# Attention on one Trainium2 core: weighing two quarters of a unit at a time, in even steps only, and both score halves ahead of the copies on VectorE

## The chip, the cores and the metric

The kernel runs on one core of one Trainium2 chip. The metric is the device time of one execution in microseconds; less is better. Times below come from three unprofiled runs and from one profiled execution.

## The reference, cut to what matters

The reference is one transformer block over `x` (2 x 2048 x 512) with 16 heads of 32, followed by a small rotation. Nearly two thirds of the device time, and all of the change, lie in its attention:

```python
scores = jnp.einsum('bhqd,bhkd->bhqk', q / math.sqrt(HEAD_DIM), k)
scores = scores + attention_bias                 # (2, 16, 2048, 2048) float32, read once
scores = jnp.where(src_mask, -jnp.inf, scores)   # keys that are padding
probs = jax.nn.softmax(scores, axis=-1)
ctx = jnp.einsum('bhqk,bhkd->bhqd', probs, v)
```

The layer norm and the projections of q, k and v stand ahead of it; the output projection, the feed-forward part and the rotation behind it.

## The kernel before

The program is three blocks, one after the other: `phase_a` (layer norm, projections), `phase_b` (attention) and `phase_c` (the rest). Only `phase_b` is touched.

**Tiles.** A tile is 128 queries of one head against all 2048 keys: a 128 x 2048 block of scores, 1 MB, whose bias is read from HBM straight into one of eight slots of `ring`. A trip has eight tiles, one for each slot, and there are 64 trips: 512 tiles. Four tiles (512 queries of one head) are a unit. Every engine has its own instruction stream, written out by hand as `step(it, j)`: trip `it`, slot `j` from 0 to 7, tile `i = it * 8 + j`. The first trip and one behind the last are unrolled; the rest is a loop over trips. Steps with even `j` are called even here, the others odd.

**What happens to a tile.**
1. SyncE loads its bias into the ring slot, as soon as the slot's last user has been turned (L450).
2. GpSimd adds the mask penalty to the first 1856 columns in place (L478). The last 192 columns get theirs from TensorE, by a matmul with the identity (L627).
3. TensorE, step `i`: scores of the tile in two halves of 1024 columns, two matmuls for each half (L621), into the PSUM tiles `scores0` and `scores1`.
4. VectorE, step `i`: `add(it, j, 0)` and `add(it, j, 1)` (L542) add each half of the scores to the ring slot and keep the row's extreme, first in `low_part`, then in `low`. The second half reads the first's `low_part`, and waits for it by the semaphore `added`.
5. ScalarE, step `i + 1`: the exponential over 2048 columns, in place (L574).
6. TensorE, step `i + 2`: the exponentials are turned (transposed) in 16 blocks of 128 x 128, four blocks to a **quarter**, in `turn(it, j, n)` for quarters n = 0 to 3 (L655). Three PSUM banks serve four quarters: an even tile uses banks 0, 1, 2, 0, an odd one 2, 1, 0, 2. So quarter 3 always needs the bank of quarter 0 of its own tile back.
7. The turned quarters are copied from PSUM to `probT`: quarters 0 and 1 by ScalarE, behind the exponential of its step (L584), quarters 2 and 3 by VectorE (L526).
8. **Weighing** (L678): when a unit's four tiles are in `probT`, its product with the values is made, `weigh(it, j)`, in four parts. One part is four matmuls of 128 x 32 against 512 columns, which run side by side on four strips of the array (the profile counts each float32 matmul twice, so a part is 8 there). The result gathers in `bank_ctx`, which ScalarE copies out to `ctxp` (L590) and stores.

**The order around the change.** TensorE's step is: scores of half 0, of half 1, turns 0 and 1, one part of the weighing, turns 2 and 3. Waits stand ahead of the instruction that needs them, some of them a block or two early. Those that matter here:
- the last score matmul of a half waits, for half 0, for the exponential of tile `i - 2` (semaphore `exp_done`), and for half 1 for VectorE's copy of quarter 2 of the tile before (`out_dve`);
- the first score matmul of a half waits for the add of that half of tile `i - 1` (`added`);
- `turn(it, j, 2)` waits at its first block for the copy of quarter 3 of the tile before (`out_dve`), and ahead of its third block for ScalarE's copy of quarter 0 of its own tile (`pe.wait_ge(out_act, t * 2 + 1)`), since quarter 3 goes into that bank.

VectorE's step is: add half 0, copy quarter 3 of tile `i - 3`, add half 1, copy quarter 2 of tile `i - 2`. ScalarE's is: exponential of tile `i - 1`, copies of quarters 0 and 1 of tile `i - 2`, and in steps 1 and 5 of a trip the copy of `bank_ctx`. Step 0 of a trip puts a small copy of `low` in front (L573).

Of the kernel before, what the change touches and what calls it, by code (L numbers as in the profile page):

```python
# [27 lines left out]
P = 128  # L28
B, S, D, F = 2, 2048, 512, 2048
H = 16  # L30
DH = D // H
# [3 lines left out]
QT = TOK // P  # L35
# [5 lines left out]
R = 2 * QT  # L41
# [334 lines left out]
def phase_b(nc, sem, side, q_rows, k_rows, v_heads, pen_scratch, ctx_scratch, ident, sums_all, low_all):  # L376
# [9 lines left out]
    QR = KB // 4  # L386
# [4 lines left out]
    UNITS = TRIPS * 2  # L391
    assert QR * P == N
    with ExitStack() as ctx:
# [33 lines left out]
        ctx_stored = sem("ctx_stored")  # L427

        SCORED0, TURNED0, PV0 = 2 * R * CH, 4 * R, 2

        block = ctx.enter_context(nc.Block())

# [74 lines left out]
        def column(all_tiles, it, j):  # L507

            if known(it):
                return all_tiles[:, it, j:j + 1]  # L510
            return all_tiles[:, bass.ds(it, 1), j:j + 1].rearrange("p o n -> p (o n)")

        @block.vector
        def _(dve):
            nc.vector.tensor_copy(identb[:], ident[:]).then_inc(identb_ready, 1)

            def copy_quarter(it, j, n, lag):

                t, k = it * R + j - lag, (j - lag) % R
                hh, q = k // QT, k % QT  # L520
                if live(t, NT):
                    dve.wait_ge(turned, TURNED0 + t * 4 + n + 1)
                    if q == 0 and n == 2:

                        dve.wait_ge(pv_done, PV0 - 1 + (it * 2 if j == 2 else it * 2 + 1))
                    nc.vector.tensor_copy(probT[:, hh, QR * n:QR * (n + 1), q * P:(q + 1) * P],  # L526
                                          turn_bank(k, n)[:].rearrange("p (c q) -> p c q", c=QR)).then_inc(out_dve, 1)

            def add(it, j, c):

                i = it * R + j
                if live(i, NT):
                    dve.wait_ge(scored, SCORED0 + i * CH + c + 1)
                    if c == 0:
                        dve.wait_ge(masked, i + 1)
                    else:
                        dve.wait_ge(added, i * CH + c)
                        if j == 0:
                            need(dve, low_kept, it)
                    dve.nop(nofuse=True)  # L540
                    at = ring[:, j, c * CW:(c + 1) * CW]
                    nc.vector.tensor_tensor_reduce(out=at, in0=scores[c][:], in1=at, scale=-1.0,  # L542
                                                   scalar=low_part[:, j:j + 1] if c else -MASKED,
                                                   op0=ALU.add, op1=ALU.min,
                                                   accum_out=low[:, j:j + 1] if c else low_part[:, j:j + 1]).then_inc(added, 1)

            def step(it, j):
                add(it, j, 0)
                copy_quarter(it, j, 3, 3)
                add(it, j, 1)  # L550
                copy_quarter(it, j, 2, 2)

            trips(dve, step)

        @block.scalar
        def _(act):
            def load_values(it, hh):
                batch, h = it // (TRIPS // B), it % H
                act.dma_start(values[:, hh, :, :].rearrange("p k d -> p (k d)"),
                              v_heads[bass.ds(batch * H + h, 1)].rearrange("o p n -> (o p) n")).then_inc(v_in[hh], 16)  # L560

            act.sem_inc(ctx_stored, 16)
            load_values(0, 0)
            load_values(0, 1)

            def step(it, j):
                i = it * R + j
                if live(i - 1, NT):
                    k, trip = (j - 1) % R, it if j else it - 1
                    act.wait_ge(added, i * CH)  # L570
                    if j == 0:

                        nc.scalar.copy(low_all[:, bass.ds(trip, 1), :].rearrange("p o n -> p (o n)"), low[:]).then_inc(low_kept, 1)  # L573
                    nc.scalar.activation(ring[:, k, :], ring[:, k, :], ACT.Exp, bias=low[:, k:k + 1], scale=-1.0,  # L574
                                         accum_out=column(sums_all, trip, k)).then_inc(exp_done, 1)
                if live(i - 2, NT):
                    k = (j - 2) % R
                    hh, q = k // QT, k % QT
                    for n in (0, 1):
                        act.wait_ge(turned, TURNED0 + (i - 2) * 4 + n + 1)  # L580
                        if q == 0 and n == 0:

                            act.wait_ge(pv_done, PV0 - 1 + (it * 2 if j == 2 else it * 2 + 1))
                        nc.scalar.copy(probT[:, hh, QR * n:QR * (n + 1), q * P:(q + 1) * P],  # L584
                                       turn_bank(k, n)[:].rearrange("p (c q) -> p c q", c=QR)).then_inc(out_act, 1)
                unit, hh = closing(it, j), 0 if j < QT else 1
                if j % QT == 1 and live(unit, UNITS):
                    act.wait_ge(pv_done, PV0 + unit + 1)
                    act.wait_ge(ctx_stored, unit * 16 + 16)
                    nc.scalar.copy(ctxp[:], bank_ctx[:]).then_inc(ctx_copied, 1)  # L590
                    if not known(it) or it < TRIPS:
                        load_values(it, hh)
                if j % QT == 2 and live(unit, UNITS):
                    trip = it - 1
                    act.wait_ge(ctx_copied, unit + 1)
                    act.dma_start(ctx_scratch[bass.ds((trip // H) * 2 * H + hh * H + trip % H, 1)].rearrange("o p n -> (o p) n"),
                                  ctxp[:]).then_inc(ctx_stored, 16)

            trips(act, step)

        @block.tensor
        def _(pe):
# [28 lines left out]
            def free_before_turn(it, j, c):  # L631

                t = it * R + j - 2
                if live(t, NT):
                    if c == 0:
                        pe.wait_ge(exp_done, t + 1)
                    else:
                        need(pe, out_dve, t * 2 - 1)

            def turn(it, j, n):  # L640

                t, slot = it * R + j - 2, (j - 2) % R
                if n == 2 and live(t, NT):
                    need(pe, out_dve, t * 2)
                for c in range(QR):
                    if c == 2:
                        if n == 0 and live(t, NT):
                            need(pe, out_act, t * 2)
                        if n == 1:
                            copied_before_weigh(it, j)  # L650
                        if n == 2 and live(t, NT):
                            pe.wait_ge(out_act, t * 2 + 1)
                    if live(t, NT):
                        at = (QR * n + c) * P
                        last = nc.tensor.transpose(turn_bank(slot, n)[:, c * P:(c + 1) * P], ring[:, slot, at:at + P], ident[:])  # L655
                if live(t, NT):
                    last.then_inc(turned, 1)

            def weighed(it, j):
                unit = it * 2 - 2 if j < 2 else it * 2 - 1 if j < 6 else it * 2  # L660
                return (j - 2) % QT, unit, 1 if 2 <= j < 6 else 0

            def copied_before_weigh(it, j):

                n, unit, hh = weighed(it, j)
                if live(unit, UNITS):
                    pe.wait_ge(out_act if n < 2 else out_dve, (unit * QT + QT - 1) * 2 + n % 2 + 1)

            def weigh(it, j):


                n, unit, hh = weighed(it, j)
                if live(unit, UNITS) and n == 0:
                    pe.wait_ge(v_in[hh], it * 16 if j == 2 else it * 16 + 16)
                    need(pe, ctx_copied, unit)
                for c in range(4):
                    if live(unit, UNITS):
                        last = nc.tensor.matmul(bank_ctx[DH * c:DH * (c + 1), :], values[:, hh, QR * n + c, :],  # L678
                                                probT[:, hh, QR * n + c, :], start=(n == 0), stop=(n == 3))
                if live(unit, UNITS) and n == 3:  # L680
                    last.then_inc(pv_done, 1)

            def step(it, j):
                score(it, j, 0)
                score(it, j, 1)
                turn(it, j, 0)
                turn(it, j, 1)
                weigh(it, j)
                turn(it, j, 2)
                turn(it, j, 3)  # L690

            trips(pe, step)
# [427 lines left out]
```

## Time and profile before

| | |
|---|---|
| median of three runs | 3677.97 us (3676.59 to 3677.99) |
| the profiled execution | 3678.13 us |
| its span, first to last instruction | 3676.1 us |
| first to last step of the attention on VectorE | 521.4 to 2545.4 us |
| busy in the span: PE / PEld / DVE / ACT / POOL | 3436.5 / 1956.3 / 2488.7 / 1893.6 / 2077.3 us |

PE is TensorE's matmul side, PEld its weight loads, DVE is VectorE, ACT is ScalarE, POOL is GpSimd, SP is SyncE. L with a number is a line of the kernel before. In a timeline row the first number is when the first instruction of a merged group starts, the second how long the group lasts; in brackets is the idle time of the engine ahead of it and what ended that. Ends of matmuls are modelled by the profiler, so starts are the safer numbers.

### The profile page before, as it was taken

The numbers are of one execution on the slowest core, as the hardware profiler recorded it, in microseconds if no ns is written. First come the engines' busy times: TensorE is split into PE (matmuls) and PEld (weight loads), VectorE is DVE, ScalarE is ACT, GpSimd is POOL, SyncE is SP. The second block draws the span as 40 slices with busy tenths as digits, with TensorE's granted clock in tenths as the row PEclk, the third lists the DMA queues.
The fourth block names the chain that finished last, engine by engine and source line by source line (L and its number), as shares of the span: only waits on it lengthen the run. The fifth ranks groups of instructions, "written<-read, shape, count | busy, mean of one in ns | idle before, by whom it ended". The sixth has DMA issues, their size and how long they took to land. (4 is left out here: it accounts for less than half of the span.)

```text
span 3676.1 us, 61259 instructions
## 1 busy us (share of the span) xinstructions
PE 3436.5 (93%) x18338; PEld 1956.3 (53%) x18338; DVE 2488.7 (68%) x4176; ACT 1893.6 (52%) x2544; POOL 2077.3 (57%) x642
## 2 busy tenths in 40 slices
PE   6787779999999999999999999998499999999997
PEld 2333336666666666666666666665244444444443
DVE  3444449999999999999999999997333424434332
ACT  2212228888888888888888888886111111111110
POOL 0000039999999999899999899996112202201100
PEclk9898889999999999999999999999799999999999
DMA  6787789999999999999999999996612202201100
GB/s 235 231 262 249 242 311 373 349 344 347 352 394 348 352 344 351 374 367 350 343 348 350 394 348 350 349 346 218 181 42 69 69 0 68 68 19 49 46 12 12
DMA packets 291097, 906.13 MB, mean 246 GB/s; under 512 B 94208, under 2 KB 94208, under 8 KB 214272
## 3 DMA queue, kind: packets, MB, share of 16 engines
q1 hardware_dynamic: 238976, 805.14, 61.4%
q10 hardware_dynamic: 49536, 92.29, 7.3%
q0 software_dynamic: 2560, 8.39, 0.6%
q8 instruction: 12, 0.20, 0.0%
q14 instruction: 13, 0.11, 0.0%
HBM read 763.12 MB, written 142.61 MB: 246 GB/s over the span
## 5 line engine op out<-in xcount | busy, mean ns | idle before, releaser
L478 POOL TENSOR_TENSOR ring<-ring,penb 128x1856 f32<-128x1856 f32 x512 | 1904.0, 3756 | 629.3 <-DMA penb<-pen_scratch 543.6
L574 ACT ACTIVATE ring<-ring,low 128x2048 f32<-128x2048 f32 x512 | 1028.7, 2009 | 317.4 <-DVE low L542 317.4
L655 PEld LDWEIGHTS b_T<-ident,ring 128*128 128x128 f32 x8192 | 890.4, 141 | 429.7 <-DVE probT L526 426.6
L655 PE MATMUL b_T<-ident,ring 128*128 128x128 f32 x8192 | 1091.8, 276 | 2.6 <-DVE probT L526 2.6
L542 DVE CUSTOM_DVE_ANT_0 ring<-scores,ring 128x1024 f32<-128x1024 f32 x512 | 627.2, 1225 | 176.8 <-PE scores L621 154.8
L526 DVE COPY probT<-b_T 128x512 f32<-128x512 f32 x1024 | 702.6, 686 | 4.9 <-PE b_T L655 4.8
L542 DVE CUSTOM_DVE_ANT_0 ring<-scores,ring,low_part 128x1024 f32<-128x1024 f32 x512 | 652.8, 1275 | 0.4
L621 PE MATMUL scores<-keys,queries 128*128 (+1 forms) x2048 | 621.7, 425 | 21.0 <-DMA queries<-q_rows 16.6
L678 PE MATMUL bank_ctx<-probT,values 128*32 128x512 f32 x4096 | 544.9, 604 | 0.0
L584 ACT COPY probT<-b_T 128x512 f32<-128x512 f32 x1024 | 538.0, 575 | 3.0 <-PE b_T L655 3.0
L845 POOL TENSOR_TENSOR y_out<-rot_a,rot_b 128x512 f32<-128x512 f32 x32 | 41.6, 1299 | 785.9 <-DVE rot_b L1003 785.9
L897 ACT ACTIVATE gate<-c_up,b_scaled 128x512 f32<-128x512 f32 x128 | 87.9, 687 | 741.1 <-PE c_up L1054 741.0
L1054 PE MATMUL c_up<-hT,w 128*128 (+1 forms) x1024 | 459.1, 592 | 0.7 <-ACT hT L889 0.7
L1064 PE MATMUL c_acc<-w,hidden 128*128 128x512 f32 x1024 | 458.9, 592 | 0.0
L621 PEld LDWEIGHTS scores<-keys,queries 128*128 128x128 f32 x2048 | 347.5, 190 | 143.6 <-DVE probT L526 74.2
L984 DVE SCALAR_TENSOR_TENSOR hidden<-c_up,b_col,gate 128x512 f32<-128x512 f32 x128 | 96.0, 750 | 393.3 <-ACT gate L897 376.5
L1064 PEld LDWEIGHTS c_acc<-w,hidden 128*128 128x128 f32 x1024 | 194.0, 190 | 241.6 <-issue 241.6
L1054 PEld LDWEIGHTS c_up<-hT,w 128*128 128x128 f32 x1024 | 190.7, 190 | 222.0 <-issue 221.0
L233 ACT ACTIVATE std<-mean_var,eps_a 128x4 f32<-128x4 f32 x8 | 2.4, 297 | 314.6 <-DVE mean_var L303 314.6
L838 POOL TENSOR_TENSOR parts<-parts 128x1024 f32<-128x1024 f32 x30 | 72.6, 2419 | 158.8 <-DMA parts<-ctx_scratch 158.7
L328 DVE TENSOR_SCALAR exact<-a_G,bias_col 128x512 f32<-128x512 f32 x64 | 48.1, 751 | 153.2 <-PE a_G L370 153.2
L1035 PE MATMUL c_fore<-wo,ctxT 128*128 128x512 f32 x256 | 116.7, 601 | 18.2 <-DVE ctxT L937 18.2
(101 smaller groups left out, 1940.2 us busy)
## 6 DMA issues: line engine op xcount, KB each, us to landing
ring<-in_fside_Bx16xSxS SPq DMA_DIRECT2D x512, 1024.0 KB, 7.5
keys<-k_rows SPq DMA_DIRECT2D x64, 1024.0 KB, 8.6
values<-v_heads ACTq DMA_DIRECT2D x128, 256.0 KB, 5.3
queries<-q_rows SPq DMA_DIRECT2D x128, 256.0 KB, 8.0
ctx_scratch<-ctxp ACTq DMA_DIRECT2D x128, 256.0 KB, 6.6
parts<-ctx_scratch SPq DMA_DIRECT2D x128, 256.0 KB, 4.9
k_rows<-part_hi SPq DMA_DIRECT2D x64, 256.0 KB, 2.9
k_rows<-part_lo SPq DMA_DIRECT2D x64, 256.0 KB, 2.9
```

Of the source, the lines that this page charges most:

```text
L478: nc.gpsimd.tensor_tensor(ring[:, j, 0:POOL_MASKED], ring[:, j, 0:POOL_MASKED], penb[:, j, 0:POOL_MASKED], ALU.add).then_inc(masked, 1)
L526: nc.vector.tensor_copy(probT[:, hh, QR * n:QR * (n + 1), q * P:(q + 1) * P], turn_bank(k, n)[:].rearrange("p (c q) -> p c q", c=QR)).then ...
L542: nc.vector.tensor_tensor_reduce(out=at, in0=scores[c][:], in1=at, scale=-1.0, scalar=low_part[:, j:j + 1] if c else -MASKED, op0=ALU.add, ...
L574: nc.scalar.activation(ring[:, k, :], ring[:, k, :], ACT.Exp, bias=low[:, k:k + 1], scale=-1.0, accum_out=column(sums_all, trip, k)).then_ ...
L584: nc.scalar.copy(probT[:, hh, QR * n:QR * (n + 1), q * P:(q + 1) * P], turn_bank(k, n)[:].rearrange("p (c q) -> p c q", c=QR)).then_inc(ou ...
L621: last = nc.tensor.matmul(scores[c][:, n * N:(n + 1) * N], queries[:, hh, q * P:(q + 1) * P], keys[:, bass.ds(it % 2, 1), c * CW + n * N:c ...
L655: last = nc.tensor.transpose(turn_bank(slot, n)[:, c * P:(c + 1) * P], ring[:, slot, at:at + P], ident[:])
L678: last = nc.tensor.matmul(bank_ctx[DH * c:DH * (c + 1), :], values[:, hh, QR * n + c, :], probT[:, hh, QR * n + c, :], start=(n == 0), sto ...
L984: nc.vector.scalar_tensor_tensor(out=hidden[:, f % 4, :], in0=up[f % 2][:], scalar=b1_col[:, f:f + 1], in1=gate[:, f % 2, :], op0=ALU.add, ...
L1035: last = nc.tensor.matmul(fore[t % 2][:], ctxT[:, c, t * P:(t + 1) * P], wo[:, c, :], start=(c == 0), stop=(c == DB - 1))
L1054: last = nc.tensor.matmul(up[f % 2][:], w1[:, c, f * P:(f + 1) * P], hT[:, bass.ds(u % 2, 1), c, :].rearrange("p o n -> p (o n)"), start=( ...
L1064: last = nc.tensor.matmul(acc[t][:], hidden[:, k % 4, t * P:(t + 1) * P], w2[:, k, :], start=(k == 0), stop=(k == FB - 1))
```

## The change

Three things move; what is computed stays the same.

- **Weighing.** `weigh` is called in even steps only, between `turn(it, j, 2)` and `turn(it, j, 3)`, and does two parts (16 matmuls in the profile's count) at once. Slots 2 and 6 do parts 0 and 1 of a unit, slots 4 and 0 do parts 2 and 3. The waits for it move into quarter 2's turn, ahead of its third block.
- **VectorE** does `add` of half 0, `add` of half 1, then copies quarter 2 and quarter 3, both of tile `i - 2`. Nothing stands between the two adds any more, and quarter 3 is copied one step earlier than before.
- **ScalarE** has its copies in a helper of its own; its order is unchanged.

```diff
@@ VectorE
             def step(it, j):
                 add(it, j, 0)
-                copy_quarter(it, j, 3, 3)
                 add(it, j, 1)
-                copy_quarter(it, j, 2, 2)
+                copy_quarter(it, j, 2)
+                copy_quarter(it, j, 3)
@@ TensorE, in turn(it, j, n)
                     if c == 2:
                         if n == 0 and live(t, NT):
                             need(pe, out_act, t * 2)
-                        if n == 1:
+                        if n == WEIGH_AFTER and j % 2 == 0:
                             copied_before_weigh(it, j)
                         if n == 2 and live(t, NT):
                             pe.wait_ge(out_act, t * 2 + 1)
@@ TensorE, the weighing
+                unit, hh, n = weighed(it, j)
                 if live(unit, UNITS):
-                    pe.wait_ge(out_act if n < 2 else out_dve, (unit * QT + QT - 1) * 2 + n % 2 + 1)
+                    if n == 0:
+                        pe.wait_ge(v_in[hh], it * 16 if j == 2 else it * 16 + 16)
+                        need(pe, ctx_copied, unit)
+                    pe.wait_ge(out_act if n == 0 else out_dve, (unit * QT + QT) * 2)
...
+                unit, hh, first = weighed(it, j)
+                for n in (first, first + 1):
+                    for c in range(4):
+                        if live(unit, UNITS):
+                            last = nc.tensor.matmul(bank_ctx[DH * c:DH * (c + 1), :], values[:, hh, QR * n + c, :],
+                                                    probT[:, hh, QR * n + c, :], start=(n == 0), stop=(n == 3))
@@ TensorE, step
                 turn(it, j, 0)
                 turn(it, j, 1)
-                weigh(it, j)
                 turn(it, j, 2)
+                if j % 2 == 0:
+                    weigh(it, j)
                 turn(it, j, 3)
```

TensorE, step 2 of a trip in the loop, from the second block of turn 1 on, before. L655 are the turns with the bank they write, L678 the weighing, L621 the next step's scores; names in brackets are the semaphores that an instruction waits for.

```order
L655 MATMUL b_T1<-ident,ring 128x128 x2
L667 ISA
L655 MATMUL b_T1<-ident,ring 128x128 [waits out_act]
L655 MATMUL b_T1<-ident,ring 128x128
L678 MATMUL bank_ctx<-probT,values 32x512 [waits ctx_copied,v_in1]
L678 MATMUL bank_ctx<-probT,values 32x512 x3
L655 MATMUL b_T2<-ident,ring 128x128 [waits out_dve]
L655 MATMUL b_T2<-ident,ring 128x128
L652 REGISTER_ALU
L655 MATMUL b_T2<-ident,ring 128x128 [waits out_act]
L655 MATMUL b_T2<-ident,ring 128x128
L655 MATMUL b_T0<-ident,ring 128x128 x4
```

The same place with the change (its lines are some ten higher: L664 the turns, L688 the weighing):

```order
L664 MATMUL b_T2<-ident,ring 128x128 [waits out_dve]
L664 MATMUL b_T2<-ident,ring 128x128
L491 REGISTER_ALU [waits v_in1]
L680 ISA [waits ctx_copied]
L661 REGISTER_ALU [waits out_act]
L664 MATMUL b_T2<-ident,ring 128x128 [waits out_act]
L664 MATMUL b_T2<-ident,ring 128x128
L688 MATMUL bank_ctx<-probT,values 32x512 x8
L664 MATMUL b_T0<-ident,ring 128x128 x4
```

The weighing is now eight matmuls in one piece, and the wait for ScalarE's copy of quarter 0, which stood behind the weighing, stands ahead of it.

VectorE, one step of the loop before (L542 the adds, L526 the copies):

```order
L535 REGISTER_ALU [waits scored]
L542 ISA ring,low_part<-scores0,ring 128x1024 [waits masked]
L542 ISA low_part 128x1
L522 REGISTER_ALU
L526 COPY probT<-b_T0 128x4x128 [waits turned]
L533 REGISTER_ALU
L537 REGISTER_ALU [waits scored]
L542 ISA ring,low<-scores1,ring,low_part 128x1024 [waits added]
L542 ISA low 128x1
L522 ISA
L526 COPY probT<-b_T0 128x4x128 [waits turned]
```

The same with the change (L543 the adds, L527 the copies):

```order
L536 REGISTER_ALU [waits scored]
L543 ISA ring,low_part<-scores0,ring 128x1024 [waits masked]
L543 ISA low_part 128x1
L534 REGISTER_ALU
L538 REGISTER_ALU [waits scored]
L543 ISA ring,low<-scores1,ring,low_part 128x1024 [waits added]
L543 ISA low 128x1
L523 ISA
L527 COPY probT<-b_T0 128x4x128 [waits turned]
L523 REGISTER_ALU
L527 COPY probT<-b_T2 128x4x128 [waits turned]
```

The copy that stood between the two adds now stands last, and the second of the copies waits for a quarter that TensorE turns, in even steps, behind the weighing of the same step.

## Rows read from the trace of the kernel before

**Rows 1.** Windows in the attention: length, busy (count) by engine, PEclk, DMA share, GB/s

```profile
1000.00:1500.00 500.00, 500.00 (x3673) 322.91 (x3665) 460.63 (x760) 406.56 (x554) 470.16 (x127) 1.00 0.96 357
2000.00:2500.00 500.00, 500.00 (x3673) 322.96 (x3666) 460.60 (x760) 406.49 (x555) 469.83 (x127) 1.00 0.96 356
```

**Rows 2.** Line L542 on VectorE: duration ns min/median/max, first and last start us

```profile
L542 DVE CUSTOM_DVE_ANT_0 ring<-scores,ring x512: 1224/1225/1227, 521.4 to 2543.7; 128x1024 f32<-128x1024 f32 x171
```

**Rows 3.** Waits by releaser, 1000 to 2500 us: us in total, times, longest

```profile
PEld b_T L655 <- DVE probT L526: 318.6, 380, 0.8
ACT ring L574 <- DVE low L542: 224.1, 333, 0.9
DVE ring L542 <- PE scores L621: 106.8, 343, 0.4
POOL ring L478 <- DMA ring<-in_fside_Bx16xSxS: 63.3, 58, 2.6
PEld scores L621 <- DVE probT L526: 54.9, 285, 0.2
```

**Rows 4.** Timeline of one step, all engines: start us, us, what [idle before]

```profile
1505.97 1.28 DVE L542 CUSTOM_DVE_ANT_0 ring<-scores,ring,low_part 128x1024 f32<-128x1024 f32 x1
...
1507.17 0.69 DVE L526 COPY probT<-b_T 128x512 f32<-128x512 f32 x1
...
1507.29 1.18 PE L621 MATMUL scores<-keys,queries 128*128 x4
1507.38 2.01 ACT L574 ACTIVATE ring<-ring,low 128x2048 f32<-128x2048 f32 x1 [0.77 <-DVE low L542]
...
1508.23 1.23 DVE L542 CUSTOM_DVE_ANT_0 ring<-scores,ring 128x1024 f32<-128x1024 f32 x1 [0.38 <-PE scores L621]
...
1508.31 0.26 PE L627 MATMUL scores<-penb,identb 128*128 128x192 bf16 x1
...
1508.41 1.04 PE L655 MATMUL b_T<-ident,ring 128*128 128x128 f32 x8
...
1509.37 1.07 PE L678 MATMUL bank_ctx<-probT,values 128*32 128x512 f32 x8
1509.38 1.05 ACT L584 COPY probT<-b_T 128x512 f32<-128x512 f32 x2
...
1509.38 0.69 DVE L526 COPY probT<-b_T 128x512 f32<-128x512 f32 x1
1509.98 1.28 DVE L542 CUSTOM_DVE_ANT_0 ring<-scores,ring,low_part 128x1024 f32<-128x1024 f32 x1
1510.37 0.86 PEld L655 LDWEIGHTS b_T<-ident,ring 128*128 128x128 f32 x8 [0.84 <-DVE probT L526]
1510.37 1.09 PE L655 MATMUL b_T<-ident,ring 128*128 128x128 f32 x8
...
1511.18 0.69 DVE L526 COPY probT<-b_T 128x512 f32<-128x512 f32 x1
...
1511.22 1.21 PE L621 MATMUL scores<-keys,queries 128*128 x4
```

**Rows 5.** The same timeline, the next step's last score load and what follows it

```profile
1511.92 0.19 PEld L621 LDWEIGHTS scores<-keys,queries 128*128 128x128 f32 x1 [0.20 <-DVE probT L526]
...
1512.27 0.10 PEld L627 LDWEIGHTS scores<-penb,identb 128*128 128x128 bf16 x1 [0.16 <-issue]
```

**Rows 6.** Timeline of VectorE in the first trip, where no copy is due between the adds

```profile
531.36 1.22 DVE L542 CUSTOM_DVE_ANT_0 ring<-scores,ring 128x1024 f32<-128x1024 f32 x1 [1.10 <-issue]
532.51 0.08 DVE L542 DVE_READ_ACCUMULATOR2_ANT low_part<- 128x1 f32 x1
532.73 1.28 DVE L542 CUSTOM_DVE_ANT_0 ring<-scores,ring,low_part 128x1024 f32<-128x1024 f32 x1
```

**Rows 7.** Groups by line, whole execution: busy us, mean ns | idle before

```profile
L584 ACT COPY probT<-b_T 128x512 f32<-128x512 f32 x1024 | 538.0, 575 | 3.0 <-PE b_T L655 3.0
L573 ACT COPY low_all<-low 128x8 f32 x64 | 12.6, 198 | 59.2 <-DVE low L542 59.2
L478 POOL TENSOR_TENSOR ring<-ring,penb 128x1856 f32<-128x1856 f32 x512 | 1904.0, 3756 | 629.3 <-DMA penb<-pen_scratch 543.6 <-DMA ring<-in_fside_Bx16xSxS 83.0
```

**Rows 8.** Timeline at the attention's end: several weighing parts in one piece, loads of each four

```profile
2554.45 0.13 PEld L678 LDWEIGHTS bank_ctx<-probT,values 128*32 128x32 f32 x4 [0.30 <-issue]
...
2556.60 0.13 PEld L678 LDWEIGHTS bank_ctx<-probT,values 128*32 128x32 f32 x4 [0.30 <-issue]
```

More of the change, by code:

```diff
@@ L429, in phase_b @@
         SCORED0, TURNED0, PV0 = 2 * R * CH, 4 * R, 2
+        WEIGH_AFTER = 2
         block = ctx.enter_context(nc.Block())
@@ L515, in _, with copy_quarter @@
             nc.vector.tensor_copy(identb[:], ident[:]).then_inc(identb_ready, 1)
-            def copy_quarter(it, j, n, lag):
-                t, k = it * R + j - lag, (j - lag) % R
+            def copy_quarter(it, j, n):
+                t, k = it * R + j - 2, (j - 2) % R
                 hh, q = k // QT, k % QT
@@ L564, in _, with exponentials @@
             load_values(0, 1)
-            def step(it, j):
+            def exponentials(it, j):
                 i = it * R + j
@@ L575, in step, with copy_quarter @@
                                          accum_out=column(sums_all, trip, k)).then_inc(exp_done, 1)
+            def copy_quarter(it, j, n):
+                i = it * R + j
                 if live(i - 2, NT):
@@ L578, in step @@
                     hh, q = k // QT, k % QT
[L579 to L585, printed above, removed]
+                    act.wait_ge(turned, TURNED0 + (i - 2) * 4 + n + 1)
+                    if q == 0 and n == 0:
+                        act.wait_ge(pv_done, PV0 - 1 + (it * 2 if j == 2 else it * 2 + 1))
+                    nc.scalar.copy(probT[:, hh, QR * n:QR * (n + 1), q * P:(q + 1) * P],
+                                   turn_bank(k, n)[:].rearrange("p (c q) -> p c q", c=QR)).then_inc(out_act, 1)
+            def step(it, j):
+                exponentials(it, j)
+                copy_quarter(it, j, 0)
+                copy_quarter(it, j, 1)
                 unit, hh = closing(it, j), 0 if j < QT else 1
@@ L636, in free_before_turn @@
                         pe.wait_ge(exp_done, t + 1)
-                    else:
+                    if c == 1:
                         need(pe, out_dve, t * 2 - 1)
@@ L660, in weighed @@
                 unit = it * 2 - 2 if j < 2 else it * 2 - 1 if j < 6 else it * 2
-                return (j - 2) % QT, unit, 1 if 2 <= j < 6 else 0
+                return unit, 1 if 2 <= j < 6 else 0, 0 if j % QT == 2 else 2
             def copied_before_weigh(it, j):
-                n, unit, hh = weighed(it, j)
+                unit, hh, n = weighed(it, j)
                 if live(unit, UNITS):
-                    pe.wait_ge(out_act if n < 2 else out_dve, (unit * QT + QT - 1) * 2 + n % 2 + 1)
+                    if n == 0:
+                        pe.wait_ge(v_in[hh], it * 16 if j == 2 else it * 16 + 16)
+                        need(pe, ctx_copied, unit)
+                    pe.wait_ge(out_act if n == 0 else out_dve, (unit * QT + QT) * 2)
             def weigh(it, j):
[L672 to L680, printed above, removed]
+                unit, hh, first = weighed(it, j)
[4 more added lines that the diff above has]
+                                                    probT[:, hh, QR * n + c, :], start=(n == 0), stop=(n == 3))
+                if live(unit, UNITS) and first == 2:
                     last.then_inc(pv_done, 1)
```

## The prediction

> **What bounds the kernel now.** The chain that ended last lies wholly in the last third, so for the attention I go by windows, waits and one step of the timeline. The windows [rows 1] show the attention steady: matmuls in progress all the time, VectorE 0.92 busy, GpSimd 0.94, the DMA engines 0.96, TensorE's clock at 1.00 of full speed, that is 2.4 GHz. The first adds run from 521.4 to 2543.7 us, 512 of them [rows 2], so a step takes 2022.3 / 511 = 3.96 us. The single step shown [rows 4] takes 3.93, from scores at 1507.29 to scores at 1511.22. In it TensorE has no gap: scores 1.02 us (to 1508.31), the masked columns 0.10, eight turns 0.96, the weighing 1.00, eight turns 0.85. The wait "PEld on DVE, 0.84" ahead of the second turns [rows 3, 4] is no loss: VectorE's copy of 1509.38 ended at 1510.07, and the loads began at 1510.37, when the matmuls of the weighing were through. A true wait is the load of the last score matmul at 1511.92, 0.05 us behind the end (1511.18 + 0.69) of VectorE's copy [rows 4, 5]. It costs little: from scores to masked columns takes 1.05 us there and 1.02 in the step before. So TensorE bounds, by a small margin: GpSimd needs 3.76 us a step [rows 7], and 0.96 of 3.96 us is 3.80 for the DMA.
>
> What matters next is how near the other loop is, in which the same engines wait for each other. For two steps it now reads: scores to first add 0.94 (1507.29 to 1508.23), first to second add 1.75 (1508.23 to 1509.98), second add to exponential 1.41 (1505.97 to 1507.38), exponential to the first copy 2.00, the copy 0.57 [rows 7] and 0.05 to TensorE, which then may make the third block of quarter 2 and five more, some 0.64, and start scores. That is 7.36 us in two steps of 7.91, so 0.55 of slack. The trace agrees: ScalarE's copy ended at 1509.38 + 0.57 = 1509.95, and its quarter's third block was due near 1510.5.
>
> **TensorE alone.** Of two steps with 2 x 1.00 us of weighing one block of 1.86 stays: 1.00 for the first part, and 2 x 0.43 for the second, since in the pile at the end six groups of four loads start 2554.45 to 2556.60, 0.43 apart [rows 8]. With one entry and one restart less (eight turns up to the weighing take 0.96 where seven spacings of 0.11 are 0.77; eight behind it last 1.09, others 1.04) two steps save about 0.14 + 0.19 - 0.11 + 0.06 = 0.28 us. By itself that would be 0.14 us a step.
>
> **VectorE's order.** Four instructions a step as before. Between the adds no copy hides the wait for `low_part`. In the first trip no copy was due there: 531.36 to 532.73, 1.37 us [rows 6], of which 1.15 is up to the reading of the accumulator. With the copy between it is 1.75, so the second add, and the exponential behind it, come 0.38 earlier. The price is 0.22 us of idle VectorE, whose own step becomes 1.37 + 1.20 + 0.60 + 0.60 = 3.77 us, still below 3.96. By the Trainium skill (VectorE: DVE Perf Modes, "The DRAIN you can't avoid") a semaphore between VectorE's operations costs nothing extra. Then first to second add would be 1.15, and the forecast below 56 us less. The row shows 1.37, and it decides.
>
> **The loop that I expect to bind.** TensorE obeys its waits in program order. In an even step the third block of quarter 2 still waits for ScalarE's copy of quarter 0, and that wait now stands ahead of the weighing, of quarter 3 and of the next step's scores. ScalarE makes that copy behind the exponential of the preceding odd step's tile, which needs that tile's adds, and those need its scores, which TensorE starts only when the even step before is through. Over a pair, from the odd step's scores to the next odd step's:
> - scores to first add 0.94, first to second add 1.37 [rows 4, 6];
> - second add to exponential 1.41, exponential to copy 2.00, copy 0.57, to TensorE 0.05 [rows 4, 5, 7];
> - two turns and the entry of the weighing: 0.96 for eight less six at 0.11, and 0.05 for the restart, 0.35;
> - the weighing, two parts: 1.86;
> - quarter 3 and the way to the scores: 0.85 for eight less four at 0.11, 0.41.
>
> Sum 8.96, and 0.05 for the copy of `low` (0.20 once in four pairs) [rows 7]: 9.01 us a pair, 4.50 a step. The adds came 0.38 earlier, but 1.86 + 0.41 of TensorE stand where 0.64 stood. 256 pairs x 9.01 = 2307 us against 512 x 3.96 = 2027 now: +280. The profiled execution took 3678.13 us, within 0.2 of the median, so 3958 us. All other edits cost nothing: ScalarE's order is the same, `bank_ctx` is finished a step earlier, quarter 3's copy is asked for a step later, and VectorE's wait for quarter 3 in even steps (it comes at the step's end) is covered, since its next add has to wait 0.94 us for scores and the copy takes 0.60 until the next start. GpSimd and the DMA will have slack: 3.76 and 3.80 of 4.50.
>
> **Bounds.** First to second add: the lower end is 1.15 (no price at all, -56 us), the upper 1.75 (as now with a copy, +97); I take 1.37, the same two instructions in this order. The waits in the loop read registers, which in the first trip were constants, so a little more is likelier than less. The weighing: 4 x 0.43 = 1.72 at least (-36), 2 x 1.00 at most (+36). The two ends far out seldom meet; that gives 3870 to 4020 for this case.
>
> **Rivals.**
> 1. **Only the bank loop binds.** If the wait for quarter 0's copy does not hold back the weighing (it is met earlier than I think, or does not keep the later matmuls), the next loop goes through VectorE: scores to first add 0.94, 1.37, add to copy of quarter 2 1.20, copy 0.69 and 0.05, load of the last score matmul to the masked columns 0.35 [rows 5], 0.10, twelve turns 0.96 + 0.44, weighing 1.86, 0.41: 8.37 us a pair, 4.19 a step, +116: 3794 us. For it: ScalarE has 0.55 us of slack today. Against: that slack is smaller than the 1.6 us that the even step adds. The Trainium skill (TensorE: Matmul & The Clock Gate, "The mechanism") has matmuls start strictly in order, only loads run ahead; by that the weighing can't pass the waiting turn. 7 in 100.
> 2. **TensorE stays the bound, and it gets faster.** The place is the same wait. If ScalarE's copy of quarter 0 lands before the third block of quarter 2 in every even step, two steps cost 7.91 - 0.28 and some 0.03 for the score wait that goes: 7.60, or 3.80 a step, where the DMA's 3.80 also stands, -81: 3597 us. For it: the exponential starts 0.38 us earlier. Against: the loop of 9.01 us would have to be 1.4 shorter; it decides at 7.91, and no term is doubtful by so much. 6 in 100. No change at all would need the loops to meet 7.91 by chance: 1 in 100.
> 3. **The clock falls too.** TensorE would stand idle some 1.4 of 9 us. The clock is 1.00 in the steady windows, which have no pause [rows 1], so they do not show what pauses do. Were a fifth of the attention at the 1.2 GHz level, TensorE's 3.6 us on the loop (0.94, 0.35, 1.86 and 0.41) would double there: 256 x 0.2 x 3.6 = +184 on top, some 4140 us. 4 in 100.
>
> **The numbers.** Likeliest case 82 in 100, 3958 us. The range 3860 to 4020 holds nearly all of it, some 80 in 100; the rivals stay outside. A measurement of this kernel tells about 0.2% from no change. Faster by more 0.06, within 0.01, slower 0.93.
>
> **What will show it.** Odd steps' scores to even steps' about 2.9 us, even to odd about 6.1 in place of 3.96 each. TensorE waits for ScalarE's `probT` copies some 0.5 us or more in each even step, a wait that is absent now, and for VectorE at the even steps' scores. First to second add 1.37 us. GpSimd idle waiting for the ring, DMA share near 0.84. It is wrong if steps alternate without a wait for ScalarE's copies (rival 1 or 2), or if the clock leaves 1.00 (rival 3).

## The result and the profile after

The changed kernel takes 3960.4 us (median of four runs, 3959.2 to 3963.57) against 3678.0 for the kernel before: ratio 1.077, 95% interval 1.0751 to 1.0789. The forecast was 3958. The whole loss lies in the attention. Its first adds on VectorE, one a tile, run from 521.6 to 2825.1 us, which is 2303.5 us where it was 2022.3 [rows 2]: 281 of the 282 us.

```profile
L543 DVE CUSTOM_DVE_ANT_0 ring<-scores,ring x512: 1212/1224/1226, 521.6 to 2825.1; 128x1024 f32<-128x1024 f32 x171
```

By the same figures the attention was 55% of the execution of the kernel before, less than the nearly two thirds named at the top.

A window in the attention of the changed kernel (length, busy and count of PE, PEld, DVE, ACT, POOL, then PEclk, DMA share, GB/s):

```profile
1000.00:1500.00 500.00, 470.66 (x3218) 288.70 (x3219) 410.84 (x665) 360.04 (x485) 413.09 (x112) 1.00 0.81 313
```

Against [rows 1] every engine does less in the same time: 112 bias tiles pass GpSimd in 500 us where 127 did, and the busy time of VectorE, ScalarE, GpSimd and the weight loads falls in about that ratio, by 11 or 12%. TensorE's matmul side counts 3218 matmuls for 3673, but its busy time falls by 6% only, because matmuls that wait for their loads count as in progress: the scores at 1501.85 below last 1.76 us, those at 1507.81 1.18. The clock stays at 1.00. No engine bounds; they wait for each other. Its waits in the attention, 1000 to 2500 us (us in total, times, longest):

```profile
POOL ring L479 <- DMA ring<-in_fside_Bx16xSxS: 232.5, 148, 3.3
DVE probT L527 <- PE b_T L664: 217.0, 167, 1.4
...
PEld b_T L664 <- ACT probT L588: 149.6, 333, 0.7
PEld b_T L664 <- issue: 140.0, 167, 0.8
...
PE b_T L664 <- ACT probT L588: 67.4, 167, 0.5
...
PEld scores L630 <- DVE probT L527: 52.1, 125, 0.4
PEld scores L630 <- DVE low L543: 47.1, 125, 0.4
```

Of [rows 3] the turns' wait of 0.84 us for VectorE, which the weighing's matmuls had filled, is still there behind each weighing: 167 times instead of 380, now put down to "issue", and no loss now either. What is new is that TensorE's loads wait for ScalarE's copies, 333 times, once in each step, and that in every second step (167 times) the matmul side itself runs dry, for 0.40 us. The largest wait, GpSimd's for the bias, is a result and no cause: its slots are loaded again only when TensorE has turned them, and it falls to 141.2 us in e1 below, where only a wait of TensorE is moved.

One pair of steps in the timeline, all engines (start us, us, what; in brackets the idle time before and what ended it). The odd step's scores are at 1498.83, the even step's at 1501.85, the next odd step's at 1507.81:

```profile
1498.83 0.70 PE L630 MATMUL scores<-keys,queries 128*128 x2
...
1499.77 1.23 DVE L543 CUSTOM_DVE_ANT_0 ring<-scores,ring 128x1024 f32<-128x1024 f32 x1
...
1501.15 1.28 DVE L543 CUSTOM_DVE_ANT_0 ring<-scores,ring,low_part 128x1024 f32<-128x1024 f32 x1
1501.21 0.64 PEld L664 LDWEIGHTS b_T<-ident,ring 128*128 128x128 f32 x6 [0.26 <-ACT probT L588]
...
1501.85 1.76 PE L630 MATMUL scores<-keys,queries 128*128 x4
...
1502.36 1.28 DVE L527 COPY probT<-b_T 128x512 f32<-128x512 f32 x2
1502.49 0.19 PEld L630 LDWEIGHTS scores<-keys,queries 128*128 128x128 f32 x1 [0.37 <-DVE low L543]
1502.56 2.00 ACT L576 ACTIVATE ring<-ring,low 128x2048 f32<-128x2048 f32 x1 [0.41 <-DVE low L543]
1503.10 0.19 PEld L630 LDWEIGHTS scores<-keys,queries 128*128 128x128 f32 x1 [0.42 <-DVE probT L527]
...
1504.56 1.05 ACT L588 COPY probT<-b_T 128x512 f32<-128x512 f32 x2
...
1505.17 0.20 PEld L664 LDWEIGHTS b_T<-ident,ring 128*128 128x128 f32 x2 [0.62 <-ACT probT L588]
...
1505.55 1.92 PE L688 MATMUL bank_ctx<-probT,values 128*32 128x512 f32 x16
...
1507.40 0.66 PE L664 MATMUL b_T<-ident,ring 128*128 128x128 f32 x4
...
1507.81 1.18 PE L630 MATMUL scores<-keys,queries 128*128 x4
```

This is the loop of the prediction, hop by hop: scores 1498.83, first add 1499.77, second add 1501.15, exponential 1502.56, ScalarE's copy 1504.56, the third block of quarter 2 at 1505.17, weighing 1505.55, quarter 3 1507.40, scores 1507.81. The pair takes 8.98 us where two steps took 7.91. TensorE's loads are held at three places of the even step, for the second add (0.37), for the copy of quarter 2 (0.42) and for ScalarE's copy (0.62), and at one of the odd step, for ScalarE's copy (0.26), but only the wait at 1505.17 lies on the loop.

### The profile page after: what moved, and what is told of

It is laid out like the page before. It is cut to its first block and busy times, and to the rows that moved or that the text cites. A ratio compares the mean times of both kernels' runs of the same rounds, so it can differ in the third digit from the quotient of the medians.

```text
span 3958.3 us, 61072 instructions
## 1 busy us (share of the span) xinstructions
PE 3583.4 (91%) x18338; PEld 1983.5 (50%) x18338; DVE 2523.4 (64%) x4176; ACT 1911.3 (48%) x2544; POOL 2075.6 (52%) x642
## 5 line engine op out<-in xcount | busy, mean ns | idle before, releaser
L664 PE MATMUL b_T<-ident,ring 128*128 128x128 f32 x8192 | 1146.3, 278 | 110.3 <-ACT probT L588 104.0
L664 PEld LDWEIGHTS b_T<-ident,ring 128*128 128x128 f32 x8192 | 884.7, 141 | 444.3 <-ACT probT L588 228.1
L527 DVE COPY probT<-b_T 128x512 f32<-128x512 f32 x1024 | 681.1, 686 | 332.5 <-PE b_T L664 332.5
L630 PE MATMUL scores<-keys,queries 128*128 (+1 forms) x2048 | 717.2, 442 | 47.7 <-DMA queries<-q_rows 16.0
L543 DVE CUSTOM_DVE_ANT_0 ring<-scores,ring,low_part 128x1024 f32<-128x1024 f32 x512 | 657.5, 1284 | 76.0 <-DVE low_part L543 11.0
L543 DVE CUSTOM_DVE_ANT_0 ring<-scores,ring 128x1024 f32<-128x1024 f32 x512 | 624.6, 1220 | 18.9 <-PE scores L630 12.3
L688 PE MATMUL bank_ctx<-probT,values 128*32 128x512 f32 x4096 | 492.3, 598 | 0.1
L688 PEld LDWEIGHTS bank_ctx<-probT,values 128*32 128x32 f32 x4096 | 107.1, 109 | 196.4 <-issue 196.4
```

Of the source, the lines that this page charges most:

```text
L630: last = nc.tensor.matmul(scores[c][:, n * N:(n + 1) * N], queries[:, hh, q * P:(q + 1) * P], keys[:, bass.ds(it % 2, 1), c * CW + n * N:c ...
```

## The experiments

Ten kernels were run. The ratio to the kernel before is given with its 95% interval.

### The wait behind the weighing (e1)

In even steps, the wait for ScalarE's copy of quarter 0 stands ahead of quarter 3, which needs its bank, and no longer ahead of the third block of quarter 2:

```diff
-                        if n == 2 and live(t, NT):
+                        if n == 2 and j % 2 == 1 and live(t, NT):
                             pe.wait_ge(out_act, t * 2 + 1)
@@ turn(it, j, n), ahead of its first block
+                if n == 3 and j % 2 == 0 and live(t, NT):
+                    pe.wait_ge(out_act, t * 2 + 1)
```

> The changed kernel, with the wait for ScalarE's copy of quarter 0 moved, in even steps, from the third block of quarter 2 (ahead of the weighing) to the first block of quarter 3 (behind it). Theory (that wait carries the loss): the loop of 8.98 us a pair goes, the next one, through VectorE's copy of quarter 2 and the last score matmul, has 8.37, so some 3795 us. Rival 1 (VectorE's adds without a copy between them are what costs): no change from the changed kernel, 3960. Rival 2 (a weighing in one long block costs by itself): 3960 as well.

Measured: 3802.04 us, ratio 1.0336 (1.032 to 1.0351). Of the 282 us lost 158 come back by moving one wait. Both rivals said 3960 and fall. TensorE's loads in an even step of this kernel:

```profile
1504.68 0.19 PEld L630 LDWEIGHTS scores<-keys,queries 128*128 128x128 f32 x1 [0.37 <-DVE low L543]
1505.28 0.19 PEld L630 LDWEIGHTS scores<-keys,queries 128*128 128x128 f32 x1 [0.42 <-DVE probT L527]
...
1505.64 1.32 PEld L666 LDWEIGHTS b_T<-ident,ring 128*128 128x128 f32 x12
1507.12 0.16 PEld L690 LDWEIGHTS bank_ctx<-probT,values 128*32 128x32 f32 x8 [0.17 <-issue]
```

Twelve blocks are now turned without a pause, and the weighing follows them. The waits that are left are the scores' for VectorE, and the second of them, for the copy of quarter 2, carries the next loop. That is rival 1 of the prediction, which had 8.37 us a pair and 3794 us; in this trace the odd steps' scores at 1501.02 and 1509.39 are 8.37 apart. That this wait carries it is shown by e8 below.

### The two parts between turns 1 and 2 (e4), and the scores' wait moved to the turns (e5, e8)

e4 puts the double block where the single one stood before:

```diff
                 turn(it, j, 1)
-                turn(it, j, 2)
                 if j % 2 == 0:
                     weigh(it, j)
+                turn(it, j, 2)
                 turn(it, j, 3)
```

> The changed kernel, with the two parts of the weighing between turns 1 and 2 of the even steps, where one part stood before. The wait for quarter 0's copy is then covered by the weighing. Theory: the loop through ScalarE has some 7.0 us a pair and does not bind; the loop through VectorE's copy of quarter 2 does, as it holds the weighing wherever it stands behind the last score matmul: 8.4 us a pair, 3795 to 3825 us. Rival 2 (the long block costs by itself): 3960.

Measured: 3838.77 us, ratio 1.0435 (1.0419 to 1.0451). The theory's direction holds, and its range ends 14 us too low. TensorE of e4, from an odd step's scores to the next odd step's:

```profile
1500.52 1.17 PE L630 MATMUL scores<-keys,queries 128*128 x4
...
1503.53 1.86 PE L630 MATMUL scores<-keys,queries 128*128 x4
1505.23 0.26 PE L636 MATMUL scores<-penb,identb 128*128 128x192 bf16 x1
...
1506.29 1.92 PE L688 MATMUL bank_ctx<-probT,values 128*32 128x512 f32 x16
1508.15 1.09 PE L664 MATMUL b_T<-ident,ring 128*128 128x128 f32 x8
1508.99 0.71 PE L630 MATMUL scores<-keys,queries 128*128 x2
```

and VectorE of e4:

```profile
1500.37 1.29 DVE L527 COPY probT<-b_T 128x512 f32<-128x512 f32 x2 [0.83 <-PE b_T L664]
1501.57 1.22 DVE L543 CUSTOM_DVE_ANT_0 ring<-scores,ring 128x1024 f32<-128x1024 f32 x1
...
1502.94 1.28 DVE L543 CUSTOM_DVE_ANT_0 ring<-scores,ring,low_part 128x1024 f32<-128x1024 f32 x1
...
1504.15 1.28 DVE L527 COPY probT<-b_T 128x512 f32<-128x512 f32 x2
...
1508.93 0.69 DVE L527 COPY probT<-b_T 128x512 f32<-128x512 f32 x1 [0.92 <-PE b_T L664]
```

In order of time: scores 1500.52, adds 1501.57 and 1502.94, copy of quarter 2 from 1504.15 to 1504.84, masked columns 1505.23, weighing 1506.29, turns 1508.15, scores 1508.99: 8.47 us, and 8.54 in the mean of all pairs (first adds from 522.8 to 2705.6). The theory missed the first hop. The first add starts 1.05 us after the scores, not 0.94, because it does not wait for them. It waits for VectorE's two copies in front of it. Both quarters are now turned behind the weighing (turns at 1508.15, copies from 1508.93), and the copies take 1.20 us up to the add (1500.37 to 1501.57). So in e4 the loop leads from those turns through both copies to the adds and back through the copy of quarter 2. The changed kernel turns quarter 2 ahead of the weighing and does not have this loop.

e5 is e4, and e8 is e1, each with the wait for the copy of quarter 2 where the bank is needed:

```diff
@@ ahead of the last score matmul of half 1
-                    if c == 1:
-                        need(pe, out_dve, t * 2 - 1)
@@ turn(it, j, n), ahead of its first block
+                if n == 0 and live(t, NT):
+                    need(pe, out_dve, t * 2 - 1)
```

> As e4 (two parts between turns 1 and 2, 3839 us), and the wait for VectorE's copy of quarter 2 stands ahead of turn 0, which needs that bank, in place of ahead of the last score matmul. Theory (e4 is held by the loop through that copy): the way from the copy's end to turn 0 falls from 0.05 + 0.35 + 0.10 to some 0.10 us, and the scores no longer wait, so 0.35 to 0.4 us a pair, 90 to 100 us: some 3735 to 3750 us. Rival (the long block or something else holds e4): no change, 3839.

Measured: 3747.77 us, ratio 1.0187 (1.017 to 1.0204), 91 us below e4. Here the copy of quarter 2 holds nothing any more: it ends at 1502.61 + 0.69 = 1503.30, and the turns' loads start at 1503.41, right behind that of the masked columns (1503.39). Of the scores' waits for VectorE only the one for its second add is left, 69.6 us from 1000 to 2500 us.

> As e1 (wait for quarter 0's copy behind the weighing, 3802 us), and the wait for VectorE's copy of quarter 2 ahead of turn 0, as in e5. Theory: 0.35 to 0.4 us a pair less, 3700 to 3712 us, still slower than before, since the loop through that copy holds a block of 1.86 us. Rival: no change, 3802.

Measured: 3709.6 us, ratio 1.0084 (1.0067 to 1.0101), 92 us below e1. VectorE and TensorE's loads of e8 in one pair:

```profile
1500.65 1.23 DVE L543 CUSTOM_DVE_ANT_0 ring<-scores,ring 128x1024 f32<-128x1024 f32 x1
...
1503.23 1.28 DVE L527 COPY probT<-b_T 128x512 f32<-128x512 f32 x2
...
1508.64 1.23 DVE L543 CUSTOM_DVE_ANT_0 ring<-scores,ring 128x1024 f32<-128x1024 f32 x1
```

```profile
1503.37 0.30 PEld L630 LDWEIGHTS scores<-keys,queries 128*128 128x128 f32 x2 [0.37 <-DVE low L543]
1503.94 0.10 PEld L636 LDWEIGHTS scores<-penb,identb 128*128 128x128 bf16 x1 [0.27 <-issue]
1503.97 1.30 PEld L666 LDWEIGHTS b_T<-ident,ring 128*128 128x128 f32 x12
```

The pair takes 7.99 us (first adds at 1500.65 and 1508.64), against 7.91 before. Two paths reach the turns at nearly one time. The copy of quarter 2 ends at 1503.23 + 0.69 = 1503.92, and the turns' loads start 0.05 behind it. The scores of half 1 had waited for VectorE's second add up to 1503.37, and what follows them, masked columns at 1503.94 and then the turns, would have put the loads at 1503.95 or 1503.96 even without the copy (behind the odd step's masked columns at 1508.72, where no copy is waited for, they come 0.01 later). So the loop still leads from VectorE's second add to the turns, and this trace does not tell by which of the two. With both waits at their latest places the joined weighing is 30 us behind the kernel before, though it saves TensorE matmul time: the block of two parts takes 1.86 us in one piece (e4: 1506.29 to 1508.15), and it stands whole on every loop that passes through the even step.

### Only the weighing's part of the change (e2)

VectorE keeps its old order, with a copy between the adds; all else as changed.

> Only the weighing's part of the change: VectorE keeps its old order (a copy between the adds). Theory: the same loop with 1.75 us between the adds in place of 1.38, so 9.35 to 9.45 us a pair, 4055 to 4080 us, slower than the whole change. Rival 1 (VectorE's order costs): near 3678, at most 3700.

Measured: 4070.31 us, ratio 1.1068 (1.1051 to 1.1085). That fits the theory's number, but the trace shows that another loop made it. TensorE of e2, an even step and the odd one behind it:

```profile
1499.63 1.44 PE L630 MATMUL scores<-keys,queries 128*128 x4
...
1502.48 0.66 PE L664 MATMUL b_T<-ident,ring 128*128 128x128 f32 x4 [0.44 <-DVE probT L527]
1503.07 1.92 PE L688 MATMUL bank_ctx<-probT,values 128*32 128x512 f32 x16
...
1505.34 1.17 PE L630 MATMUL scores<-keys,queries 128*128 x4
...
1508.17 1.09 PE L664 MATMUL b_T<-ident,ring 128*128 128x128 f32 x8 [0.69 <-DVE probT L527]
1509.02 1.45 PE L630 MATMUL scores<-keys,queries 128*128 x4
```

Here quarter 2's turn waits in every step for the copy of quarter 3 of the tile before, which the old order puts between the adds: 2.85 us from the scores to that turn in the even step and 2.83 in the odd one. That makes 5.71 + 3.68 = 9.39 us a pair, as much as the loop through ScalarE would with 1.75 us between the adds (9.35 to 9.45). But ScalarE's loop does not hold this kernel. Its waits from 1000 to 2500 us have this row, one wait a step:

```profile
PE b_T L664 <- DVE probT L527: 176.6, 317, 0.7
```

They have none for ScalarE's copies; in the whole execution TensorE's matmul side waited for one of those once, 0.8 us. In the even step shown, ScalarE's copy had landed at 1502.65, when the third block of quarter 2 was due at 1502.70. So the agreement with the forecast of 4055 to 4080 us is chance: the theory's loop was nearly as long, and one that the expectation did not name came first. What the run shows is that VectorE's new order is worth 110 us beside the new weighing, and that it is no part of the loss.

### More work on ScalarE, after and before (e6a, e6b)

A copy of 128 x 128 elements that feeds nothing stands ahead of each exponential.

```diff
+                    nc.scalar.copy(spare[:, k, :], ident[:])
                     nc.scalar.activation(ring[:, k, :], ring[:, k, :], ACT.Exp, bias=low[:, k:k + 1], scale=-1.0,
```

> The changed kernel with a copy of 128 x 128 elements (it feeds nothing) ahead of each exponential on ScalarE, by the rows for 8 and 512 columns some 0.29 us long, of which some 0.22 to 0.25 us delay what follows. Theory (ScalarE's exponential and copy lie on the loop once in a pair): 256 times that, 56 to 64 us over the changed kernel's 3960: 4016 to 4024 us. Rival (ScalarE has slack, the loss is elsewhere): 3960.

Measured: 3996.68 us, ratio 1.0865 (1.0846 to 1.0883), 36 us over the changed kernel.

> The same extra copy in the kernel before. Theory: its loop through ScalarE has 0.55 us of slack in a pair and takes 0.22 to 0.25 of it: no change, 3678, at most 3688. Rival (ScalarE's time counts anyway): 3735 to 3800.

Measured: 3678.53 us, ratio 1.0001 (0.9992 to 1.0011). In the kernel before the same copy costs nothing; in the changed one it shows, but with 0.14 us a pair, not 0.22 to 0.25. The rows of e6a, VectorE's second add and ScalarE behind it:

```profile
1502.63 1.28 DVE L544 CUSTOM_DVE_ANT_0 ring<-scores,ring,low_part 128x1024 f32<-128x1024 f32 x1
```

```profile
1503.96 0.30 ACT L577 COPY spare<-ident 128x128 f32<-128x128 f32 x1 [0.53 <-DVE low L544]
1504.16 2.00 ACT L578 ACTIVATE ring<-ring,low 128x2048 f32<-128x2048 f32 x1
```

From the add to the small copy it is 1.33 us where it was 1.41 to the exponential, and the exponential starts 0.20 behind the copy's start: 1.53 against 1.41, so 0.12 of the 0.14 measured. The sign is as the theory has it, and the rival's 3960 falls; the size was estimated wrongly.

### Only VectorE's part of the change (e3), and what it gains (e9, e7)

e3 is the kernel before, with both adds ahead of the copies:

```diff
                 add(it, j, 0)
-                copy_quarter(it, j, 3, 3)
                 add(it, j, 1)
                 copy_quarter(it, j, 2, 2)
+                copy_quarter(it, j, 3, 2)
```

> Only VectorE's part of the change: both adds, then its copies; the weighing stays as before. Theory: TensorE stays the bound; the last score matmul's wait for VectorE's copy of quarter 2, worth some 0.02 us a step, goes: 3665 to 3678 us. Rival 1 (VectorE's order costs, by 0.22 us of idle VectorE a step): 3790 if it came at full price, or 3960 if it is the whole loss.

Measured: 3664.84 us, ratio 0.9962 (0.9949 to 0.9976): faster than before, by 14 us. e9 is the kernel before, with only the wait for the copy of quarter 2 moved to turn 0, the edit of e5 and e8:

> The kernel before with one edit: the wait for VectorE's copy of quarter 2 stands ahead of turn 0 in place of ahead of the last score matmul. Theory (that wait costs some 0.02 us a step, and e3 gained by ending it): it goes here too, 3665 to 3671 us, as e3's 3665. Rival (e3 gained by something else in VectorE's order): 3678.

Measured: 3665.68 us, ratio 0.9968 (0.9956 to 0.9979). e7 has both edits:

> e3 (only VectorE's part of the change, 3665 us) with the edit of e9 as well. Theory: the wait is already met in e3, so nothing more: 3662 to 3668 us. Rival (more is left in that wait): below 3660.

Measured: 3664.23 us, ratio 0.9965 (0.9951 to 0.9978). Either edit brings the same 0.3 to 0.4%, and both together bring no more, as they would if both end one and the same wait. That wait, of the scores for the copy of quarter 2, was 54.9 us from 1000 to 2500 us [rows 3]; it is 17.0 us in e3 and gone in e9 and e7. The first adds of e3, then of e9:

```profile
L542 DVE CUSTOM_DVE_ANT_0 ring<-scores,ring x512: 1211/1215/1226, 522.5 to 2530.3; 128x1024 f32<-128x1024 f32 x171
L542 DVE CUSTOM_DVE_ANT_0 ring<-scores,ring x512: 1223/1225/1226, 521.3 to 2530.7; 128x1024 f32<-128x1024 f32 x171
```

That is 2007.8 and 2009.4 us where it was 2022.3 [rows 2], or 3.93 us a step for 3.96. These three are the versions that beat both kernels.

## Why the prediction was right

**The loop.** Forecast and measured, hop by hop: 0.94 and 0.94; 1.37 and 1.38; 1.41 and 1.41; 2.00 and 2.00; copy and way to TensorE 0.62 and 0.61; to the weighing 0.35 and 0.38; weighing 1.86 and 1.85; quarter 3 to scores 0.41 and 0.41. The sum was 8.96 and is 8.98; with the copy of `low` it was 9.01 and is 9.02 in the mean. The forecast lay 2 us below the result. That it was so near is partly luck: the hops were rounded to 0.01 us, and 0.01 us in a pair is 2.6 us in the whole. Six of the eight hops could be read off a step of the kernel before. The one between the adds came from the first trip, where the same two instructions happened to stand without a copy between them, and the weighing was worked out from one part and the spacing in the pile at the end.

**That it binds through that wait** is shown by e1 (158 us back for moving it), in which nothing else changes, and by e6a beside e6b (time added on ScalarE counts in the changed kernel and not in the one before). In the changed kernel the weighing never passes the waiting turn: it starts 0.38 us behind the load that waited. e2 does not count as support, since another loop held it.

**The next loop**, rival 1, was worked out as 8.37 us a pair and 3794 us for the case that the wait did not hold the weighing; e1 measured 3802. e8 confirms its path: 92 us, or 0.36 a pair, for taking 0.35 us a pair off the way from VectorE's copy to the turns. e5 does the same for e4's loop, with 91.

**A semaphore between VectorE's operations.** The row of 1.37 us was taken against the Trainium skill's statement (VectorE: DVE Perf Modes, "The DRAIN you can't avoid") that the semaphore costs nothing extra, which the page has measured on eight copies in a row. Between the adds the wait does cost: 1.38 us from add to add in the changed kernel, 1.15 from an add to a copy that needs nothing of it (e2 on VectorE):

```profile
1506.28 1.23 DVE L543 CUSTOM_DVE_ANT_0 ring<-scores,ring 128x1024 f32<-128x1024 f32 x1 [2.05 <-PE scores L630]
...
1507.43 0.69 DVE L527 COPY probT<-b_T 128x512 f32<-128x512 f32 x1
```

That copy waits for a semaphore too, `turned`, which was raised long before, and that costs nothing, as the page has it. The second add waits for a result that the first has only just written. By the page's rule applied to it the forecast would have been 56 us lower, and the row decided rightly.

**What was missed** changed nothing in the sum. The odd step takes 3.02 us, not 2.9, for TensorE waits 0.26 us for ScalarE's copy there too: turn 0 done, a copy of 0.57 us, and six more blocks take less than that. The pair with the copy of `low` takes 9.12 us, so that copy costs 0.14 us once in four pairs, not 0.20. The DMA share fell to 0.81, not 0.84. TensorE was to stand idle some 1.4 us of the 9; its matmul side shows 0.53 (88 of 1500 us in 167 pairs), because the other waits lie inside matmuls that count as in progress. The clock stayed at 1.00, so rival 3 had nothing behind it.

**Faster, rival 2,** would have needed the loops to be shorter than TensorE's own time. e8 has the two waits as late as the banks allow, and is still 0.8% slower than before, and 1.2% slower than e7, which has VectorE's new order and the late wait but the old weighing.

## What to carry to other kernels

Before moving work on one engine, follow each wait around its whole loop, through the other engines and back, over as many steps as the new order repeats in; the hops can be read in the trace of the old kernel even where they are hidden. Joining two short blocks into one saves their entries but puts the double block whole on each loop that passes through that step; the other step does not give back what the loop lost. And look where a wait stands relative to what needs it: a wait placed a few instructions early cost 0.3% in the kernel before, and another one 4% in the changed one. A number that comes out as forecast does not show that the loop behind it is the right one: in e2 it was another, and only the list of waits told.

## What the runs showed of the hardware that was not expected

- ScalarE's small copy of 0.30 us ahead of a waiting exponential delayed it by 0.12 us only (0.14 a pair by the time of e6a): the first operation behind the wait starts 0.08 us sooner than the exponential did, and the next one 0.20 us after it.
- A wait shown as 0.2 us on TensorE's load side cost about a sixth of that in time. The scores' wait for VectorE's copy stood in three of four steps of the kernel before, 54.9 us in 380 steps or 0.14 us a step [rows 3]; ending it (e9), or most of it (e3), gave 12 to 14 us in 512 steps, 0.02 to 0.03 us each.
